# A tenth embedding table by one-hot matmul in place of a gathered one, with a smaller DMA scratch

## The reference

```python
e = stack([tbl_f[ids[:, f]] for f in range(26)], axis=1)      # (2048, 26, 128)
combined = concatenate([dense[:, None, :], e], axis=1)        # (2048, 27, 128)
G = einsum('bfd,bgd->bfg', combined, combined)                # all pairs of features
z = concatenate([dense, G[:, iu, ju]], axis=1)                # upper triangle, 351 pairs
h = concatenate([z, dense], axis=1)                           # 607 columns
h = maximum(h @ W_top1 + b_top1, 0)                           # 512
h = maximum(h @ W_top2 + b_top2, 0)                           # 256
y = h @ W_top3                                                # (2048, 1)
```

## Time and profile before

| what | value |
|---|---|
| median of three runs | 563.65 us (563.34 to 564.11) |
| profiled execution, first to last instruction (span) | 563.2 us |
| median of the runs less that span | 0.45 us |
| instructions | 9906 |
| DMA moved | 36.73 MB, mean 65 GB/s |
| gathers (GpSimd indirect DMAs) | 272 |
| mean granted TensorE clock | 0.839 |

### The profile page before, as it was taken

The page is one execution under the profiler, slowest core; times in us unless marked ns, Lnnn a source line. Parts: engine busy times, 40 slices in busy tenths (PEclk is TensorE's granted clock), DMA queues, the critical chain, the costliest instruction groups (busy, mean ns, idle before and its releaser), DMA issues.

```text
span 563.2 us, 9906 instructions
## 1 busy us (share of the span) xinstructions
PE 409.3 (73%) x4248; PEld 375.3 (67%) x4248; DVE 251.8 (45%) x340; ACT 142.7 (25%) x370; POOL 258.4 (46%) x280
## 2 busy tenths in 40 slices
PE   2477564759785696875859468595885848868998
PEld 1466564759583694875849368585885748857987
DVE  4579243844431654353444344445442354424322
ACT  3263111422121221221122121222221222212431
POOL 6736363553626536262554625546063662625200
PEclk9868695969887698787979689798797968879899
DMA  7954521231212212031212212222121221211000
GB/s 186 246 129 104 178 62 43 61 80 39 57 29 76 74 45 56 25 91 43 56 48 60 68 44 57 47 55 74 25 66 38 72 61 35 65 34 48 21 11 1
DMA packets 20132, 36.73 MB, mean 65 GB/s; under 512 B 6157, under 2 KB 9877, under 8 KB 20090
## 3 DMA queue, kind: packets, MB, share of 16 engines
q0 software_dynamic: 8704, 17.84, 12.4%
q1 hardware_dynamic: 5338, 9.08, 6.3%
q10 hardware_dynamic: 6048, 9.18, 6.2%
HBM read 36.07 MB, written 0.01 MB: 64 GB/s over the span
## 4 chain that ended last, share of the span: by engine, by line
PE 58%; issue 16%; another core or an unknown queue 16%; DVE 6%; ACT 3%; DMA 1%; SPq 0%; DVEq 0%; ACTq 0%
PE psB L424 19%; PE psG L450 15%; PE psB L499 7%; PE psB L506 5%; PE psB L408 5%; DVE one_hot L724 3%; PE psB L493 2%; DVE tab_lo L736 2%; PE psB L511 1%; ACT ET L627 1%; DMA oidx<-hot_idx 1%; PE psB L478 1%; PE psB L475 1%; ACT ET L647 1%
## 5 line engine op out<-in xcount | busy, mean ns | idle before, releaser
L349 POOL DMA_INDIRECT E<-tbl,gidx x272 | 257.5, 947 | 266.3 <-PE psB L408 156.3
L724 DVE TENSOR_TENSOR one_hot<-oidx,psR 125x1024 fp32r<-125x1024 int32 (+1 forms) x152 | 178.0, 1190 | 189.5 <-remote 135.7
L450 PE MATMUL psG<-ET 128*52 128x52 f32 x2048 | 93.3, 263 | 79.1 <-issue 55.7
L450 PEld LDWEIGHTS psG<-ET 128*52 128x52 f32 x2048 | 84.2, 175 | 88.8 <-issue 76.0
L424 PE MATMUL psB<-one_hot,tab_hi 125*128 125x256 f32 x592 | 112.5, 314 | 24.3 <-ACT tab_hi L594 10.9
L424 PE MATMUL psB<-one_hot,tab_lo 125*128 125x256 f32 x592 | 104.5, 300 | 7.2 <-issue 5.1
L424 PEld LDWEIGHTS psB<-one_hot,tab_hi 125*128 125x128 f32 x592 | 89.8, 208 | 29.6 <-issue 20.9
L424 PEld LDWEIGHTS psB<-one_hot,tab_lo 125*128 125x128 f32 x592 | 89.3, 207 | 7.8 <-issue 4.9
L627 ACT COPY ET<-psB 128x512 f32<-128x512 f32 (+3 forms) x80 | 44.2, 570 | 86.6 <-PE psB L408 34.6
L772 DVE COPY_PREDICATED S<-second,psG 116x208 f32<-116x208 int32 x64 | 25.1, 391 | 76.5 <-ACT S L656 76.5
L656 ACT COPY S<-psG 116x208 f32<-116x208 f32 x64 | 21.3, 333 | 103.2 <-remote 52.5
(11 more groups left out here) (54 smaller groups left out, 213.4 us busy)
## 6 DMA issues: line engine op xcount, KB each, us to landing
oidx<-hot_idx ACTq DMA_DIRECT2D x28, 256.0 KB
E<-tbl,gidx POOLq DMA_INDIRECT x272
ET<-tbl SPq DMA_DIRECT2D x3, 448.0 KB
oidx<-hot_idx SPq DMA_DIRECT2D x4, 256.0 KB
dense<-dense_pairs SPq DMA_DIRECT2D x8, 128.0 KB
ZH<-tbl SPq DMA_DIRECT2D x2, 448.0 KB
S<-tbl SPq DMA_DIRECT2D x2, 448.0 KB
oidx<-hot_idx ACTq DMA_DIRECT2D x7, 128.0 KB
```

The source lines that it names most:

```text
L349: nc.gpsimd.indirect_dma_start(E[:, n % SLOTS, i, :], None, gathered[feature_and_tile(n, i)[0]], bass.IndirectOffsetOnAxis(ap=gidx[:, 4 * ...
L450: gram = nc.tensor.matmul(psG[g % 2][q * LANE:q * LANE + M, a * M:(a + 1) * M], two[:, 0:M], two[:, PAIR:], start=True, stop=True)
L724: nc.vector.tensor_tensor(one_hot[0:ROWS_P, m % RING, 0:many], ids, rows, ALU.is_equal).then_inc(hot_full[m % RING], 1)
```

## The change

- `HOT_TABLES` takes two tables of 1,250 rows: `NS` becomes 10, `NG` 16. There are 64 T groups, four in each half; 22 chunks and 168 hot matmuls a duo, 11 in each half. The number of features stays 27.
- The last fill now has two tables, its id load 256 KB.
- The tenth table is staged where the first one lay (`raw_ET`, part 0); its load waits until the first two have been copied on (`raw_ready` 2). Two tables are now split from SBUF, at steps 13 and 15 of half 0; `clear_G` moves to step 16.
- The SBUF scratch for dynamic DMAs is set to 8192 bytes a partition (it was left at the default).
- `W1_AT` and `U_AT`, positions in half 2, follow the number of chunks: 11 to 15 and 16.

```diff
-HOT_TABLES = ((1000, 8), (1250, 1))
+HOT_TABLES = ((1000, 8), (1250, 2))
+DMA_SCRATCH = 8192
...
-    W1_AT, U_AT = (9, 10, 11, 12, 13), 14
+    W1_AT, U_AT = range(CHUNKS // 2, CHUNKS // 2 + 5), CHUNKS // 2 + 5
...
-                      (raw_S, 0), (raw_S, 1), (raw_w2, 0), (raw_S[:, 2 * TABLE_K[0] * D:], 0)]
+                      (raw_S, 0), (raw_S, 1), (raw_w2, 0), (raw_S[:, 2 * TABLE_K[0] * D:], 0), (raw_ET, 0)]
+        VIA_PSUM = sum(k * D <= 2 * 512 for k in TABLE_K)
+        REUSED = NS - 1
...
             def load_table(h):
                 rows = small[h].rearrange("(p k) d -> p (k d)", k=TABLE_K[h])
+                if h == REUSED:
+                    sp.wait_ge(raw_ready, 2)
...
             def round_table(h):
-                if h < NS - 1:
+                if h < VIA_PSUM:
...
             def split_table(h):
-                if h == NS - 1:
+                if h >= VIA_PSUM:
...
-                        if step[1] == 0 and step[2] % 2 == 0 and built_tables < NS - 1:
+                        if step[1] == 0 and step[2] % 2 == 0 and built_tables < VIA_PSUM:
                             split_table(built_tables)
                             built_tables += 1
-                        if step[1:] == (0, 2 * NS - 5):
-                            split_table(NS - 1)
+                        for i in range(VIA_PSUM, NS):
+                            if step[1:] == (0, 2 * i - 3):
+                                split_table(i)
...
-    nc = _bacc.Bacc("TRN2", target_bir_lowering=False, num_devices=1)
+    nc = _bacc.Bacc("TRN2", target_bir_lowering=False, num_devices=1,
+                    dynamic_dma_scratch_size=DMA_SCRATCH)
```

## The result

The changed kernel takes 549.67 us (four runs, 548.43 to 551.06) against 563.88 (563.34 to 566.63) before; the ratio is 0.9753, 95% interval [0.972, 0.9786]. Timed again on another chip it was 549.12 against 562.76, 0.9742 [0.971, 0.9774]. It is 2.5% faster. 558.8 was forecast, with a range down to 551.0: the sign was right, the size was not, and the time lies just outside the range. It is rival 3's time (551.3) within 0.3%.

What follows compares the result with a forecast made beforehand. TensorE's completions were taken to be held back during GpSimd's gather bursts. The terms: 563.2 - 10.8 + 7.5 - 1.6 = 558.3 us of span, 558.8 with the median 0.45 above; 8-in-10 range 551 to 570.

Steps and rivals of the forecast that it cites:

- rival 3: Added matmuls are hidden wholly and the bursts alone set the halves: 551.3 us; chance 0.14.
- How much of it shows? ... I take 0.45: +7.5 us: Behind the head, 16.7 us of added one-hot matmuls on TensorE show at 0.45: +7.5 us, bounds 0 and +16.7.
- the head: Up to the first gram's merge: one gather group fewer, the tenth table's builds and split more; -1.6 us, bounds -4 and +4.5.
- The gathers' term: Halves 4, 8, 12 lose their fifth gather group, -13.8 us; the halves behind give back 3.0; net -10.8.
- SP's new wait: On SP's queue, the wait for the first two tables' copies (`raw_ready` 2) was forecast to cost nothing.
- Rival 1: Bursts break apart: in odd halves late groups make gathers pause again, slower, 570 us; chance 0.17.
- Rival 4: Gathers cost nothing but their transposes, TensorE's order alone sets the end: +17.3, 581 us; chance 0.04.
- The scratch: The smaller scratch for gather descriptors was taken to cost 0; as rival 5, throttling gathers, +26 us, chance 0.03.

Runs made afterwards that it cites:

- the kernel with doubled chunks: The kernel before with chunks 2, 7 and 16 of seven duos multiplied twice, 154 matmuls or 18.4 us more: 561.3 us, 0.9959 of the kernel before.
- paced: The changed kernel with each half's 16 gathers evenly spread, each waiting for a step a sixteenth of the half's TensorE work later: 457.38 us, 0.8143 of the kernel before.

## Why the prediction was wrong

**The step that failed** is "How much of it shows? ... I take 0.45: +7.5 us". The added matmuls cost nothing: the ten other halves hold 12 of the 21 added chunks, 9.5 of the 16.7 us, and came out 0.95 us shorter, and 18.4 us of matmuls put into the kernel before left it at 0.9959 [0.9922, 0.9997]. That is well shown for the odd halves, which got 16 of the 20 a duo. In the even halves little was added on balance (4), and there taking 17 a half out did save their price in halves 4 to 12. Rival 3, which had 0.14, was the case. The mechanism had been read correctly in the same text, "a half-duo is its gathers plus what TensorE does outside the bursts"; the price then went against it. The comparison that gave the 0.45 (half 1 against half 7, four layer parts more for 2.6 us) measured something else. By their timelines half 1 has a lead of 5.7 us, a block of 22.2 and a tail of 1.4, half 7 has 8.0, 21.5 and 2.4. The 2.6 us are lead and tail; a chunk placed between two T groups is in neither. The first layer part stands ahead of the half's first T group, in the lead; the other three lie between groups, in the block. It had to be asked where the parts lie, not how many there are. The test was at hand: in the trace of before the block is 21.45 to 21.54 us in every 16-gather half from 2 to 13, whatever TensorE has to do in it. By the spans this step is 8.4 of the 11.7 us by which the forecast (558.3) was above 546.6; the head is 1.9, the halves behind the long ones 1.2, the long ones 0.2. By the times the forecast was 9.1 above: 0.45 was taken for what the median lies above the span, and it is 3.1.

**The gathers' term** was right in kind and size: -14.0 in halves 4, 8 and 12 where -13.8 was written, and the kernel before with those twelve gathers left out falls by 2.2% [1.6, 2.7]. The three halves behind gave back 1.84 us, not 3.0. With the gathers left out they gave back none: they take 30.7 us there behind halves that are no longer long, so following a long half isn't why they are short. In the changed kernel halves 5 and 9 grew by 1.07 and 0.77 and half 13 not at all; why is open.

**The head** gained 3.46 us for 1.6. The last gather is issued at 59.94 and ends at 60.88 (forecast: done by 59.7), but the last chunks were not behind it: the last fill is copied at 59.49, ahead of the last gather's end, and the first merge comes 1.74 us after that end, where 2.8 had been taken from the kernel before and 2 more added for the chunks. The tenth table's load, its split from SBUF and SP's new wait delayed nothing that shows here.

**Rival 1** (bursts break apart) did not happen: group 4 still came in time, two bursts and one long pause in each half; four halves (2, 4, 9 and 12) had a further pause of 0.6 us after four gathers. Half 12 is the longest of all, 35.14, but by its lead (8.96); its block is 21.53 like the others, and the block of the ninth 21.84. The experiments also turn its sign. Half 6 of the kernel with doubled chunks had just that further pause and was shorter; with the bursts broken up 549 us fell to 457. "Bursts break apart" was priced as a cost because a pause was read as lost time for GpSimd. In these runs it was time given to TensorE.

**Rival 4**, the rule that DMA and TensorE never wait on each other, is refuted by the three long halves as the prediction said. The Trainium skill's page "SBUF — State Buffer" (section "Who interferes with whom") has it that DMA contends with no compute engine. For plain DMAs, from SP or GpSimd, the runs agree (398.1 and 396.58 us, TensorE 92% busy). Beside bursts of indirect ones TensorE's matmuls run on for a while (269.90 above), but in the end it has gaps, and the engines that wait for it stand for up to 7.2 us, so the time that the rule would give (581 as priced in rival 4) did not come, and the measurement decides.

**The scratch** costs nothing that can be told from noise, as assumed: spacing is 1.25 us still, and alone it gives 1.0034 [0.9999, 1.0069].

What stays open is why indirect DMAs hold TensorE's completions. Behind the head the runs show when (from some 4 us into a burst to 2 us past it) and that the density of the gathers matters, not which part of the chip is busy with them, nor whether it is the indirect form or how long GpSimd issues without a break. The "4 us" is no constant either: the head's first burst of 20 runs from 3.27 to 28.09 us, and the completion of a chunk whose matmuls ended at 14.5 had come through by 17.60; that of the next chunk, 1.8 us later, let VectorE on only at 28.74.

## What to carry to other kernels

When several engines that wait for one engine are released at the same moment, look at what a third engine was issuing just before, and cut the time into blocks by that; here work added inside a block was free, and work at its edges was not. Price an added piece by where it lands, not by an average over halves that differ in more than that piece. And gathers spread over the time in which they are needed were worth more than six times as much as having 16 fewer of them: 549 to 457 us, with nothing left out and no buffer added, against 564 to 550.

## What the runs showed of the hardware

- Beside indirect DMAs issued one every 1.25 us TensorE's completions came late: in half 7 waiters stood for up to 7.2 us and were released together, some 2 us after the burst's last one, though the matmuls had run some 5 us earlier. Plain DMAs of the same size, issued by SP or GpSimd, had no such effect (398.1 and 396.58 us in place of 549); those of GpSimd also kept it busy for less than half as long.
- An indirect DMA costs GpSimd 0.94 us for 128 rows and 0.90 for 64, with 0.30 between two; a plain one for 128 rows 0.54.
- The mean granted TensorE clock was 0.839 in the kernel before, 0.881 in the changed one, 0.962 in it when paced, 0.978 with plain DMAs. It doesn't follow the time alone: without most of the tenth table's matmuls it was 0.832, and that kernel was some 7 us faster than the changed one.
- A scratch for dynamic DMAs of 8192 bytes a partition in place of the default changed nothing measurable (1.0034 [0.9999, 1.0069]) in a kernel with up to twelve gathers back to back behind the head.
- The best version found is the paced one, 457.38 us (450.47 on another chip), 19% below the kernel before.
